# AdaLN attention and ternary FFN on one core: first and last batches reordered, FFN2 started unit by unit, four score banks for the last attention

## What is computed

```
xn = rms_norm(x, g_norm) * (1 + scale) + shift        # scale, shift = emb @ W_emb + b_emb
q, k, v = split(xn @ W_qkv)                            # 16 heads of 32
q = rms_norm(q, g_q);  k = rms_norm(k, g_k)
o = softmax(q @ k.T * 32 ** -0.5) @ v
y = o + o @ W_out
h = gelu(quant(layer_norm(y)) @ ternary(w_fc).T)       # 512 -> 2048
ffn = quant(layer_norm(h)) @ ternary(w_proj).T         # 2048 -> 512
out = x + ffn                                          # ternary(w): sign(round(w / mean|w|)) * mean|w|
```

## Time and profile before

| | us |
|---|---|
| median of 3 runs | 1147.8 |
| lowest, highest | 1147.66, 1148.79 |
| the profiled execution | 1148.41 |
| its span, first to last instruction | 1146.5 |
| PE busy | 1070.8 (93% of the span) |
| DVE busy | 866.2 (76%) |
| ACT busy | 812.2 (71%) |
| POOL busy | 548.8 (48%) |
| one iteration of the hardware loop | 65.0 |

### The profile page before, as it was taken

The page is one execution under the profiler, slowest core; times in us unless marked ns, Lnnn a source line. Parts: engine busy times, 40 slices in busy tenths (PEclk is TensorE's granted clock), DMA queues, the critical chain, the costliest instruction groups (busy, mean ns, idle before and its releaser), DMA issues.

```text
span 1146.5 us, 26244 instructions
## 1 busy us (share of the span) xinstructions
PE 1070.8 (93%) x9484; PEld 678.0 (59%) x9484; DVE 866.2 (76%) x1616; ACT 812.2 (71%) x1372; POOL 548.8 (48%) x365
## 2 busy tenths in 40 slices
PE   4647899999999999999999999999999999999796
PEld 1324565766666665766666665666666565666463
DVE  4668758788787878788787878788787878777444
ACT  4876676868768686877768586877868586776742
POOL 1522172644629083654719173553819174563425
PEclk8868999999999999999999999999999999999889
DMA  9810303121030313111030313112030312111101
GB/s 349 300 31 1 93 20 75 57 48 65 25 87 37 74 54 73 55 39 60 30 91 37 73 55 73 55 30 62 37 91 37 73 55 55 38 23 35 38 1 55
DMA packets 75501, 74.20 MB, mean 65 GB/s; under 512 B 6592, under 2 KB 56000, under 8 KB 74944
## 3 DMA queue, kind: packets, MB, share of 16 engines
q1 hardware_dynamic: 75456, 73.59, 21.6%
HBM read 39.89 MB, written 8.39 MB: 42 GB/s over the span
## 4 chain that ended last, share of the span: by engine, by line
PE 84%; ACT 7%; DVE 5%; issue 3%; DMA 0%; SPq 0%; ACTq 0%; DVEq 0%; POOL 0%
PE F L782 9%; PE F L783 9%; PE F L625 9%; PE F L627 9%; PE QB L593 3%; PE QB L594 3%; PE QB L595 3%; PE QA L593 3%; PE QA L594 3%; PE QA L595 3%; PE T L813 2%; PE SB L681 2%; PE SA L681 2%; PE PV L698 2%; PE PV L697 2%
## 5 line engine op out<-in xcount | busy, mean ns | idle before, releaser
L782 PE MATMUL F<-yT_hi,fc_t 128*128 128x256 f16 x1024 | 227.5, 274 | 0.0
L783 PE MATMUL F<-yT_lo,fc_t 128*128 128x256 f16 x1024 | 227.2, 273 | 0.0
L552 POOL TENSOR_TENSOR rqk<-ssq,half 128x16 f32<-128x16 f32 x64 | 186.9, 2921 | 80.1 <-DVE ssq L1241 80.1
L625 PE MATMUL F<-proj_t,hs 128*128 128x512 f16 x512 | 196.9, 385 | 3.8 <-DVE hs L1206 3.8
L627 PE MATMUL F<-proj_t,hs 128*128 128x512 f16 x512 | 196.4, 384 | 0.0
L520 POOL TENSOR_TENSOR acc<-acc,hg 128x512 f32<-128x512 f32 x96 | 153.2, 1596 | 8.6
L1206 DVE SCALAR_TENSOR_TENSOR hs<-hg,g_inv,hs 128x512 f16<-128x512 f32 x128 | 112.1, 876 | 58.6 <-ACT hs L922 58.4
L527 POOL TENSOR_TENSOR acc<-acc,hq 128x512 f32<-128x512 f32 x96 | 123.4, 1285 | 19.2 <-ACT hq L978 8.9
L1220 DVE TENSOR_TENSOR p_lo<-SA,p_hi 128x512 f16<-128x512 f32 x128 | 88.2, 689 | 45.2 <-ACT p_hi L938 45.0
L917 ACT ACTIVATE hg<-F,g_fc 128x512 f32<-128x512 f32 x128 | 87.3, 682 | 49.4 <-PE F L783 47.9
L520 POOL TENSOR_TENSOR acc<-hg 128x512 f32<-128x512 f32 x16 | 20.3, 1271 | 212.2 <-DVE hs L1206 162.2
(11 more groups left out here) (192 smaller groups left out, 2752.0 us busy)
## 6 DMA issues: line engine op xcount, KB each, us to landing
stk<-qkT SPq DMA_DIRECT2D x128, 128.0 KB, 2.5
xtok<-in_x SPq DMA_DIRECT2D x16, 512.0 KB, 3.4
xT_sb<-in_xT SPq DMA_DIRECT2D x16, 512.0 KB, 3.3
stk<-qkT SPq DMA_DIRECT2D x128, 64.0 KB, 2.1
xres<-in_x SPq DMA_DIRECT2D x16, 512.0 KB, 3.3
out<-xres SPq DMA_DIRECT2D x16, 512.0 KB, 2.8
stk<-in_w_emb SPq DMA_DIRECT2D x4, 512.0 KB, 4.9
fc_t<-in_w_qkv SPq DMA_DIRECT2D x2, 1024.0 KB, 11.0
```

What stands on the lines that cost most here:

```text
L552: pool.tensor_tensor(rqk[:, n % 2, :], ssq[:, n % 2, :], half[:, :], ALU.pow).then_inc(rqk_r, 1)
L625: pe.matmul(FB[t][:, :], hs[:, 0, k // 2, col:col + P], proj_t[:, k, :], start=(k == 0), stop=False)
L782: pe.matmul(dst, w, yT_hi[:, k, :], start=(k == 0), stop=False)
L783: mm = pe.matmul(dst, w, yT_lo[:, k, :], start=False, stop=(k == KT - 1))
```

## The change

1. **Iteration 0.** DVE's ternary passes and ACT's rounding passes come after the norms, turns and squares of the same head instead of ahead of them. ACT squares the tokens (`junk`) ahead of its magnitudes and rounding passes. DVE's `msx` moves from unit 2 to unit 7 (`msx_unit`), behind the last row maxima.
2. **Second FFN product by units.** `second` waits at every step `e` for the low part of unit `e` alone, and at the first step of tile 1 for 7 gelus instead of 8. This holds in every iteration, the loop included.
3. **Last attention (iteration 15).** Scores go to four banks (`SA`, `SB`, `QA`, `QB`) and are issued two heads ahead. PE has a table of its own, `LAST_FILLER`, with one step of the second product per place.
4. **Iteration 16.** `TAIL_FILLER` puts the whole of `PROJ1` first. ACT does only the squares of units 0 to 2 between the gelus and the other five behind the last unit. The sums of the squares go from POOL to DVE (`add_squares`, after units 5 and 7). DVE's residual of batch 14, tile 0, comes ahead of the units. PE finishes the output projection of tile 0 before it starts tile 1.
5. **Batch 15's residual** is made in `xtok`, loaded early, and written by two DMAs, one for each tile.

```diff
@@ filler, tables
+LAST_FILLER = {0: PROJ1[0:1], 1: PROJ1[1:2], 2: PROJ1[2:3], 3: PROJ1[3:4], 5: PROJ1[4:5], 7: PROJ1[5:6],
+               9: PROJ1[6:7], 11: PROJ1[7:8], 13: PROJ0[0:2]}
+TAIL_FILLER = {0: PROJ1, 12: PROJ0[0:2]}
+TAIL_SUMS = {5: (1,), 7: (2, 3, 4, 5, 6, 7)}
+def last(b):
+    return isinstance(b, int) and b == B - 1
+def msx_unit(i):
+    return UNITS - 1 if isinstance(i, int) and i == 0 else MSX_UNIT
+        def score_banks(b):
+            return SB + QB if last(b) else SB
@@ SP
+                if last(ffn):
+                    sp.wait_ge(ssx_r, nth(ffn, TT, TT))
+                    sp.dma_start(xtok[:, :, :], x_t[ffn]).then_inc(ld_last, 16)
                 if late is not None:
-                    sp.wait_ge(out_r, nth(late, TT, TT))
-                    sp.dma_start(out_t[late], xres[:, :, :]).then_inc(st_out, 16)
+                    if last(late):
+                        for t in (1, 0):
+                            sp.wait_ge(out_r, nth(late, TT, tile_no(t)))
+                            sp.dma_start(out_t[late][:, t:t + 1, :], residue(late)[:, t:t + 1, :]).then_inc(st_out, 16)
...
@@ POOL, no attention beside the FFN
                         for n in range(1, UNITS):
                             add_h(n)
-                            add_q(n)
@@ PE
                     if e == 0:
-                        pe.wait_ge(gelu_r, nth(b, UNITS, UNITS))
-                        pe.wait_ge(hlo_r, nth(b, UNITS, UNITS))
+                        pe.wait_ge(gelu_r, nth(b, UNITS, UNITS - t))
+                    pe.wait_ge(hlo_r, nth(b, UNITS, e + 1))
...
-                    if h < 2:
+                    used = h - len(score_banks(att))
+                    if used < 0:
                         pe.wait_ge(max_r, nth(att, HEADS, HEADS))
                     else:
-                        pe.wait_ge(plo_r, nth(att, HEADS, h - 1))
+                        pe.wait_ge(plo_r, nth(att, HEADS, used + 1))
...
-                        scores(h)
+                        if not last(att):
+                            scores(h)
+                        else:
+                            if h == 0:
+                                scores(0)
+                                scores(1)
+                            if h + 2 < HEADS:
+                                scores(h + 2)
@@ ACT, units
-                        if att is None:
-                            square_hidden(ffn, n)
-                        elif n in HSQ_UNIT:
+                        if n in HSQ_UNIT:
                             square_hidden(ffn, HSQ_UNIT[n])
+                if ffn is not None and att is None:
+                    for n in range(len(HSQ_UNIT), UNITS):
+                        square_hidden(ffn, n)
@@ DVE
+            def add_squares(b, n):
+                dve.wait_ge(hsq_r, nth(b, UNITS, n + 1))
+                if n > 1:
+                    dve.wait_ge(sumq_r, nth(b, UNITS - 1, n - 1))
+                else:
+                    dve.wait_ge(fold_r, nth(b - 1, 1, 1))
+                dve.tensor_tensor(acc[:, 1, :], hq[:, 0, :] if n == 1 else acc[:, 1, :], hq[:, n, :], ALU.add
+                                  ).then_inc(sumq_r, 1)
...
-                    if n == MSX_UNIT and pre is not None and not first(pre):
+                    if n == msx_unit(i) and pre is not None and not first(pre):
                         mean_square(pre)
```

More of the change, by code:

```diff
@@ L739, in iteration @@
                         pe.wait_ge(wo_h, 2)
[L740 removed]
+                    steps = [(0, k) for k in range(KT - 1)] + [(1, 0), (0, KT - 1)] + [(1, k) for k in range(1, KT)]
+                    for t, k in sorted(steps) if att is None else steps:
                         if (t, k) == (0, KT - 1):
@@ L877, in iteration @@
                     qkv_weights((2,))
-                if isinstance(i, int) and i == 0:
-                    magnitudes(1, PROJ_ABS_ORDER[2])
-                    magnitudes(1, PROJ_ABS_ORDER[3])
-                    for k in range(4):
-                        rounded(0, k)
-                    act.wait_ge(wo_i, KT)
-                    act.activation(wo_hi[:, :, :].rearrange("p k n -> p (k n)"), wo_raw, ACT.Identity,
-                                   scale=WO_SCALE).then_inc(wo_h, 1)
                 if ffn is not None:
@@ L906, in iteration @@
                                        ).then_inc(ssx_r, 1)
+                if isinstance(i, int) and i == 0:
+                    magnitudes(1, PROJ_ABS_ORDER[2])
+                    magnitudes(1, PROJ_ABS_ORDER[3])
+                    for k in range(4):
+                        rounded(0, k)
+                    act.wait_ge(wo_i, KT)
+                    act.activation(wo_hi[:, :, :].rearrange("p k n -> p (k n)"), wo_raw, ACT.Identity,
+                                   scale=WO_SCALE).then_inc(wo_h, 1)
                 if ffn is not None:
@@ L1183, in iteration @@
                     result(late, 0)
+                if late is not None and last(ffn):
+                    residual(late, 0)
                 for n in range(UNITS):
```

51 lines of the change are left out of this document (35 added, 16 removed).

## The result

| | kernel before | changed kernel |
|---|---|---|
| median | 1148.3 us (1147.66 to 1150.99) | 1129.69 us (1129.29 to 1130.82) |
| ratio, 95% interval | | 0.9833 [0.9821, 0.9846] |
| profiled execution: time, span | 1148.41 us, 1146.5 us | 1130.04 us, 1128.2 us |
| mean granted clock | 0.969 | 0.977 |

Both medians are of four executions. The forecast of 1131.4 us lay 1.7 us too high, and the time is inside the range. The page's line of busy times of the changed kernel, as the earlier trace rows: PE is busy for 6 us less with the same 9484 matmuls, since less of its work is done at the low clock, and holds 94% of a span that is 18.3 us shorter.

What follows compares the result with a forecast made beforehand. PE was taken to bound the long middle, with losses in iteration 0, the last attention and the last FFN. 3.5 + 2.4 + 5.4 + 5.2 - 0.1 = 16.4 us gave 1131.4 us, range 1127.0 to 1136.5.

Steps and rivals of the forecast that it cites:

- Start of iteration 0: Ahead of iteration 0's heads: earlier token squares bring the first `p_lo` from 73.69 to about 70.2, gaining 3.5 us.
- Heads of iteration 0: Iteration 0's heads: norms and turns ahead of the ternary passes gain 2.4 us, within bounds of 0 and 5.6.
- rival B: Iteration 0's heads give nothing beyond the start, because every `p_lo` still stands behind a pass: 1133.8 us, chance 0.10.
- Waits by unit: PE's 14 new waits in each of 15 FFN batches: 0.1 us charged, at most 0.5 us.
- Rival E: Finer waits hold PE up in every iteration, making the kernel slower, say 1152 us; chance 0.03.
- Last attention: Iteration 15's attention: ACT fed by four banks and two heads of lead gains 8.2 - 1.9 - 0.9 = 5.4 us.
- The knot: Last attention, heads 12 and 13: sums' turn and eight `PROJ0` matmuls delay head 11's values product, costing 1.9 us.
- the clock's: Last attention: PE's thinly spread work falls to the low clock level again for some microseconds, 0.9 us charged.
- Rival A: Last attention: PE mostly at the low level, gain 2.5 instead of 5.4 us, 1134.3 us; chance 0.13.
- Last FFN: Iteration 16: the 3.84 us idle and 1.74 us of low clock go, less 0.4 for the fold: 5.2 us.
- The fold: Last FFN: DVE's fold after six additions, done at 1129.6 against PE's need at 1130.1; 0.4 us late charged.
- Rival C: Last FFN: DVE and POOL hold each other up, fold 2.3 us late instead of 0.4, 1133.3 us; chance 0.10.

Runs made afterwards that it cites:

- with the start: Only the iteration 0 edit of the mean square's place and ACT's order ahead of the heads, put into the kernel before: 1145.97 us, ratio 0.9975.
- with the attention alone: Only four score banks, scores two heads ahead and proj matmuls one unit at a head in iteration 15, put into the kernel before: 1143.42 us, ratio 0.9949.
- the FFN alone: Kernel before with only the last FFN's edits, including waits by unit, sums on DVE and the residual in two stores: 1143.35 us, ratio 0.9944.
- the knot: Changed kernel with the eight proj matmuls of tile 0 at head 15 of the last attention instead of head 13: 1130.49 us, ratio 0.9833 to the kernel before.
- the late ternary pass: Changed kernel with iteration 0's last ternary pass behind head 15 instead of head 13: 1130.0 us, ratio 0.9829 to the kernel before.
- feeding: Matmuls that nobody reads, added to the changed kernel where PE waits, in three kernels: 1128.96, 1130.02 and 1126.9 us.
- two places: Changed kernel plus unread matmuls at the start of iteration 1 and behind the last four values products of the last attention: 1128.96 us, ratio 0.9818.
- three-place kernel: Changed kernel plus unread matmuls at iteration 1's start, behind the last four values products and behind head 1 of the last attention: 1130.02 us, ratio 0.983.

## Why the prediction was right, point by point

- **Start of iteration 0**, 3.5 predicted: 3.67 measured, and 3.68 alone. `wo_lo` at 66.11 for 65.7, the first exponential at 67.49 for 67.8. `wo_hi` is what caps it, as said: it ends at 66.08.
- **Heads of iteration 0**, 2.4 predicted: 3.39 measured. The hand layout was 1.0 too small, or 0.5, since kernels with the same code took 37.06 to 37.56 us there; rival B (nothing) falls. 0.61 us were lost at the low clock behind it, for which the prediction had no term; of kernels with the same code up to there two took 62.3 us for that stretch, as before, and three 62.7 to 63.0, so the change itself need not be the cause.
- **Waits by unit**, 0.1 charged: -0.05 measured over 13 iterations, and 0.2 at most by the other kernels. Rival E falls.
- **Last attention**, 5.4 predicted: 6.14 measured. The knot was forecast as 1.9 and is 1.88. The term that was mis-sized is the clock's: 0.9 charged, none paid in this stretch (1.00). That is in part luck: another execution of the same code had a clock of 0.93 there and paid just 0.90 (24.29 us), which is the forecast's figure. The reason given for the feeding was only partly right: four banks and the lead are worth 1.5 to 2.4 of it, and the rest came with the order of the proj matmuls, which the prediction did not price by itself. Rival A falls.
- **Last FFN**, 5.2 predicted: 3.50 + 1.83 = 5.33 measured. The wait of 3.84 and the low level are gone. How much of the 3.50 is the edit's is good to about 1 us, since that stretch was also 1.03 and 0.95 us shorter in the kernels with the start and with the attention alone; the FFN alone, with the clock behind the attention as before (0.83), gave 3.47 + 1.82. The fold, charged at 0.4 late, is in time, since DVE needs 4.66 us for six additions with 4.3 estimated and PE's 40 matmuls leave room for it. Rival C falls: its price was for additions beside POOL, and only one of the seven stands there, 1.75 us long beside 0.69 for the six others. By the rule that the prediction cites (the Trainium skill, SBUF — State Buffer, "Who interferes with whom") that one addition should be held up by POOL and the others not, and the trace agrees.
- **The last store**, counted as nothing: 0.7. This step failed. From the start of the last residual, with which the earlier trace rows end, to the end of the span it is 3.2 us for 3.9, since only a DMA of 256 KB stands behind it, which lands in 2.0 us where one of 512 KB takes 2.8.

The two terms left out (0.6 lost, 0.7 won) cancel. The 1.7 us by which the time came out under the forecast are in the main the 1.0 in the heads and the 0.7 in the attention; what is left (0.2 at the start, 0.1 in the FFN, 0.1 or 0.2 in the waits, against 0.36 of later start-up) is within what executions of one kernel differ by. So the mechanisms held, and the closeness of the number is in part luck: the clock moved one stretch by 0.9 us between executions of the same code.

## What to carry to other kernels

A step that is taken off the path gives back its full time only if the work behind it was waiting; look a stage further for the next engine, as the knot and the late ternary pass show, both of which moved for nothing. Where PE is busy for only part of a stretch, price its clock as a term of its own, 0.8 to 2.0 us at each such place here (what feeding gave back: 2.03 to fold 1, 1.25 behind the attention, 0.8 at its start), and expect it to lie elsewhere after any edit; measure the parts by the stretches between fixed events and not by the total alone. If such a stretch can't be filled with real work, a matmul that nobody reads in a bank that is free may pay, as it did here by 3.3 us in the profiled executions and 2.4 by the ratios. With two places it was 1.7 us by the ratios and with three 0.3, within the intervals.

## What the runs showed of the hardware

- The same last attention took 29.53, 30.43 and 31.26 us in three kernels that differ only in iteration 0, at granted clocks of 0.83, 0.83 and 0.78. Whether the edit 950 us ahead or the execution made that difference was not told apart; executions of the same code differed there by up to 0.9 us.
- The low level was not bound to a long wait: in the three-place kernel it came behind one of 1.36 us, and in the changed kernel a wait of 2.34 us was followed by 21 us at full clock. A high busy share in a stretch with the low level (4.91 of 5.00 us at 0.69) is in part made by it: matmuls of one size stood 0.43 us apart at the low level and 0.22 at the full one (output projection of iteration 16).
- A DVE addition with both inputs in SBUF took 1.75 us beside one of POOL's sums and 0.69 us without.
- 14 more semaphore waits for each batch on PE, all long met, cost 0.2 us at most over 13 iterations of 65 us.
